# An fp6 linear layer's pairs moved into the attention heads' stage of a macaron block

## The reference

```
x = x + 0.5 * moe(layernorm(x));  x = x + attention(layernorm(x));  x = x + 0.5 * moe(layernorm(x))
x = x + 0.5 * fp6_linear(layernorm(x))                       # first use
x = x + heads(layernorm(x))                                  # 16 heads, causal, relative bias, its own layernorm inside
x = x + 0.5 * fp6_linear(layernorm(x))                       # second use, same weight and bias

fp6_linear(x): for each row and block of 32: s = max(max|x| / 7.5, 1e-30); q = nearest value of the e2m3 grid to x / s
               the same for the weight's rows;  out = (q * s) @ (qw * sw).T + bias
heads(x):      xn = layernorm(x) * gamma + beta;  q, k, v = xn @ W.T;  softmax(q k / 4 + rel[dist], causal) v;  @ Wo.T
```

## Time and profile before

| | us |
|---|---|
| median of 3 runs | 2751.59 |
| lowest, highest | 2748.57, 2754.42 |
| the profiled execution | 2777.85 |
| its span, first to last instruction | 2776.0 |
| first use of the fp6 layer | 194 (1544 to 1738) |
| heads | 860 (1738 to 2598) |
| second use of the fp6 layer | 178 (2598 to 2776) |

### The profile page before, as it was taken

One profiled execution on the slowest core, in us unless ns is written; L12 is line 12 of the kernel. 1 busy time (PEld: TensorE's weight loads), 2 busy tenths in 40 slices (PEclk: granted clock), 3 DMA queues, 4 the chain that ended last, 5 costly groups with the idle time before them and its releaser, 6 DMA issues.

```text
span 2776.0 us, 39998 instructions
## 1 busy us (share of the span) xinstructions
PE 2217.6 (80%) x13342; PEld 1613.4 (58%) x13342; DVE 1620.4 (58%) x4577; ACT 969.2 (35%) x1964; POOL 453.9 (16%) x402
## 2 busy tenths in 40 slices
PE   4489999908999857999994276378999999999476
PEld 2478888806888736888883144324444454444254
DVE  6744443353555675433444897266866766875695
ACT  4122233203333331232331331325555556556321
POOL 4320000040000134000003553411011011000242
PEclk8799999958999878999997555669999999999755
DMA  7110101020000122001002100242322323230001
GB/s 237 41 59 26 28 28 32 22 76 1 1 1 1 35 83 73 28 28 32 28 28 60 49 12 0 61 65 59 48 42 53 48 47 63 37 43 2 5 22 39
DMA packets 83735, 114.14 MB, mean 41 GB/s; under 512 B 12162, under 2 KB 74020, under 8 KB 80420
## 3 DMA queue, kind: packets, MB, share of 16 engines
q1 hardware_dynamic: 77396, 94.53, 15.5%
q0 software_dynamic: 6144, 17.05, 1.9%
HBM read 68.90 MB, written 42.64 MB: 40 GB/s over the span
## 4 chain that ended last, share of the span: by engine, by line
PE 63%; DVE 21%; ACT 5%; issue 5%; DMA 3%; POOL 2%; another core or an unknown queue 1%; SPq 0%; ACTq 0%; DVEq 0%; POOLq 0%
PE psum L774 9%; PE psum L776 9%; PE psum L775 9%; PE psum L122 5%; PE psum L2097 4%; PE psum L123 4%; PE psum L124 4%; PE psum L2076 4%; PE psum L2056 3%; PE psum L861 3%; PE psum L2080 3%; DVE junk L1961 2%; PE psum L1426 2%; DVE m L1949 1%; DVE stats L155 1%
## 5 line engine op out<-in xcount | busy, mean ns | idle before, releaser
L1898 ACT ACTIVATE pt<-psum 128x512 f32<-128x512 f32 (+3 forms) x768 | 338.9, 491 | 283.2 <-DVE psum L1987 196.2
L739 DVE SCALAR_TENSOR_TENSOR h<-psum,xg,sg 128x128 f32<-128x128 f32 x592 | 166.9, 345 | 415.2 <-PE psum L861 415.2
L774 PE MATMUL psum<-w_hi,xt_hi 128*128 (+1 forms) x720 | 286.3, 398 | 33.7 <-DVE xt_lo L704 33.7
L548 ACT ACTIVATE sg<-psum 128x512 f32<-128x512 f32 x180 | 107.6, 598 | 584.0 <-PE psum L776 543.0
L775 PE MATMUL psum<-w_lo,xt_hi 128*128 (+1 forms) x720 | 284.5, 395 | 0.0
L776 PE MATMUL psum<-w_hi,xt_lo 128*128 (+1 forms) x720 | 284.5, 395 | 0.0
L2056 PE MATMUL psum<-ks,qs 96*128 96x512 bf16 (+3 forms) x768 | 232.9, 342 | 49.7 <-DMA ks<-qk_scr 19.9
L2076 PE MATMUL psum<-qs,ks 99*128 99x512 bf16 (+3 forms) x768 | 236.8, 332 | 18.4 <-ACT pt L1898 11.4
L774 PE MATMUL psum<-w_hi,ht_hi 128*128 (+1 forms) x720 | 220.5, 306 | 8.3 <-DVE x L754 8.0
L1961 DVE CUSTOM_DVE_ANT_0 junk<-psum,band_q 128x256 bf16<-128x256 f32 (+1 forms) x512 | 204.8, 400 | 22.3 <-PE psum L2056 12.0
L776 PE MATMUL psum<-w_hi,ht_lo 128*128 (+1 forms) x720 | 205.9, 286 | 0.0
(11 more groups left out here) (281 smaller groups left out, 4884.4 us busy)
## 6 DMA issues: line engine op xcount, KB each, us to landing
xg<-w_dram SPq DMA_DIRECT2D x54, 256.0 KB, 3.3
qk_scr<-parts SPq DMA_DIRECT2D x32, 384.0 KB, 2.5
qs<-qk_scr SPq DMA_DIRECT2D x96, 128.0 KB, 7.0
ks<-qk_scr SPq DMA_DIRECT2D x96, 128.0 KB, 7.7
xg<-rows_in SPq DMA_DIRECT2D x74, 132.0 KB, 2.2
rows_out<-yb SPq DMA_DIRECT2D x74, 128.0 KB, 1.7
x<-x_dram SPq DMA_DIRECT2D x4, 1024.0 KB, 9.3
out_dram<-x SPq DMA_DIRECT2D x4, 1024.0 KB, 4.4
```

The lines of the kernel that those rows point to most:

```text
L739: ins = dve.scalar_tensor_tensor(out=h[i % 2][:, e, :], in0=u[:, e, :], scalar=xg[j % XSLOT][:, at:at + 1], in1=sg[i % 2][:, e, :], op0=AL ...
L774: pe.matmul(out, a[0], b[0], start=first, stop=False)
L1898: act.activation(pt[n % NPT][:, 0:q1 - q0], st_bank(n)[:, 0:q1 - q0], ACT.Exp).then_inc(*exped.up())
```

## The change

`linear` and `linear_order` are replaced by a class `Linear` with the steps of each engine, `pair_steps` (the steps of a pair, with `slack` empty rounds in two places) and `in_turn` (the rounds). `linear_first` is the first stage with the pairs of batches 0 and 1 only, 8 pairs. The other 24 pairs, 8 of the first use for batches 2 and 3 and 16 of the second, stand in the heads' order: a `fill` with two pairs in flight and five empty rounds in each of two places gives one round after each score step. In batches 0 to 2 it begins with the third unit, in batch 3 after the last batch's output step; 6, 6, 4 and 4 pairs are dealt to the four batches, and the last 4 pairs (batch 3 of the second use) follow the heads with one empty round. A batch of the second use is stored when its fourth pair is summed. The weight is quantised once.

Two sets of buffers for the pairs are laid over those of the projection: `xn`, `xt`, `parts`, `rests`. `rests` and `yd` become one buffer, and a third of the `pt` buffers is 384 columns wide instead of 512. ScalarE waits, before a pair's centring, for the projection and the writes from `parts`; before an output step it waits for the pairs' products. The `sum` of a pair (now `lin_sum`) follows `lin` by one round, where it was three; the second rounding has steps of its own (`round`, `even`) behind the empty rounds. A batch's projection starts when the last batch's conclusion has been written, not with it. The pairs' turns and products use the heads' ring of three banks.

The roots are made per batch, at `heads_stat` and `linear_stat` in the order, with Ln and Exp in place of Sqrt and a reciprocal, and two refinements in place of one.

```
+        def pair_steps(n, layer, pair, slack):
+
+            yield [("centre", n)]
+            for kind in ("amax", "scaled", "power", "shift"):
+                yield [(kind, n)]
+            for _ in range(slack):
+                yield []
+            yield [("round", n)]
+            yield [("even", n)]
+            yield [("least", n)]
+            yield [("requant", n)]
+            for _ in range(slack):
+                yield []
+            yield [("q_turn", n)]
+            yield [("q_low", n)]
+            yield [("lin", n)]
+            yield [("lin_sum", n)]
+            yield [("lin_collect", n)] if layer == 0 else [("lin_store", n)]
...
             for u in range(NU):
                 b, g = divmod(u, NHG)
                 if g == 0:
                     proj = project(b + 1) if b + 1 < BATCH else iter(())
+                    may_project, may_fill = b == 0, False
+                if g == (2 if b + 1 < BATCH else 0):
+                    fill = linear_fill(([("linear_stat", b - 1)] if b else []) + list(mine[b]), 5)
+                    may_fill = g == 2
...
-                    order.extend(next(tail, []))
-                    if step % 3 == 0:
+                    late = next(tail, None)
+                    order.extend(late or [])
+                    may_project, may_fill = may_project or late is None, may_fill or late is None
+                    if step % 3 == 0 and may_project:
                         order.extend(next(proj, []))
+                    if may_fill:
+                        order.extend(next(fill, []))
...
+                size = TILES * D
+                words = parts[:, :, :, :].rearrange("p a k s -> p (a k s)").bitcast(F32)
+                linear.begin(jobs, [
+                    Quantising(st, flat(xn)[:, 0:size], flat(xn)[:, size:2 * size], rests[0],
+                               flat(xt[0])[:, 0:size], flat(xt[1])[:, 0:size]),
+                    Quantising(st, rests[1], words[:, 0:size], words[:, size:2 * size],
+                               flat(xt[0])[:, size:2 * size], flat(xt[1])[:, size:2 * size])], mx_ring.bank)
...
+                def inverse_root(which, b):
+
+                    at = slice(b * BT, (b + 1) * BT)
+                    act.wait_ge(*S("variance")(roots[which, b] + 1))
+                    act.activation(sd[:, at], ve[:, at], ACT.Ln).then_inc(*S("logarithm").up())
+                    act.wait_ge(*S("logarithm")(roots[which, b] + 1))
+                    act.activation(recip[:, at], sd[:, at], ACT.Exp, scale=-0.5).then_inc(*S("root").up())
...
         with ExitStack() as stack:
-            tables = HeadTables(stack)
-            linear(False, tables)
-            attention_heads(tables)
-        linear(True)
+            tables, linear = HeadTables(stack), Linear(stack)
+            linear_first(tables, linear, 2)
+            attention_heads(tables, linear, 2)
```

553 lines of the change are left out of this document (313 added, 240 removed).

## The result

The changed kernel takes 2838.09 us (median of 4 runs, 2833.51 to 2840.95); the kernel before, on the same chip, 2750.08 (2748.53 to 2754.42). The ratio is 1.0316, 95% interval 1.0296 to 1.0335: 3.2% slower, where I had forecast 0.6% faster and a range that ended at 2788.

The account below looks back on a forecast made before the run. TensorE was taken to set the pace in the heads' stage, with VectorE 81% busy. First stage -72, roots +45, fills +142, collision -17 and end -114 gave -16: 2736 us from a median of 2751.6, range 2692 to 2788.

Parts of the forecast that it names:

- First stage: First use of the fp6 layer: keeping 8 of 16 pairs saves 74 us, less 2 for the earlier sum: -72.
- Roots: Per-batch roots by Ln and Exp: +6 at the heads' start, +24 in the loop, +15 for linear roots: +45.
- Collision: Projection's write behind a unit's loads in batches 1 and 2: twice 8.33 us of waiting goes, -17.
- End: Second use's 178 us stage goes; a root, four last pairs and the store take 64 us: -114.
- Fills: Twenty pairs in four stretches of the heads' loop: +100 floor from VectorE's work, +42 for product waits: +142.
- the two prices of a pair: A moved pair in the heads' stage: VectorE 6.6 us, or 7.6 with statistics; TensorE 3.3 us at full clock.
- 2.1 us for a product's piece: In the fills, VectorE's wait for a pair's 2.8 us of products costs 2.1 us each, 20 times: +42.
- The floor case: Rival: fills cost only VectorE's work beyond its free time, -42, and -8 for a shorter end; 2694 us, chance 0.17.
- the forecast's bubbles: VectorE's waits for pairs' products in the fills, limited by three banks of maxima: +42 over twenty pairs.
- The clock rival: Rival: TensorE falls to 1.2 GHz in the fills, deciding under a mean grant of 0.77; +57, 2793 us, chance 0.15.
- The late bias additions: Rival: VectorE's late bias additions in the fills hold ScalarE, then TensorE, 0.8 us each; +40, 2776 us, chance 0.15.
- 76 us more at the worst: Over 20 pairs, GpSimd operations fully stopping VectorE, 3.8 us a pair, could cost up to 76 us more.

Follow-up runs that it names:

- e12: Changed kernel with the first use in its own stage, only eight second-use pairs moved into the heads' stage, eight in a last stage; 1.0112 of the kernel before.
- e9: Kernel before with only the next batch's projection starting after the previous unit's output step, no pair moved; 1.0039 of the kernel before.
- e8: Changed kernel with all sixteen first-use pairs back in their own stage, the second use left moved; 1.0253 of the kernel before.
- e18: Kernel before plus 216 independent VectorE maxima and, in the same eight units, three pieces a unit of twelve TensorE products; 1.0540 of the kernel before.
- e13: Kernel before plus 216 independent VectorE maxima of about 0.69 us, 27 in each of eight units; 1.0395 of the kernel before.
- e7: Changed kernel with batch 2's four second-use pairs moved from units 12 and 13 to the middle of unit 14 on; 1.0294 of the kernel before.
- e14: Changed kernel with each score product issued twice in the units with pairs; 1.0333 of the kernel before.
- e2: Changed kernel with each score product issued three times in the eight units with pairs; 1.0413 of the kernel before.
- e5: Changed kernel without VectorE's bias additions in the eight units with pairs, ScalarE taking those scores from TensorE; 1.0215 of the kernel before.

## Why the prediction was wrong, step by step

- *First stage, -72 forecast:* 194 us became 114.3, -80. Right in kind, 8 us better.
- *Roots, +45:* the start +5.3 (107.5 for the 102.2 from 1738 to before's first maxima at 1840.2); batch 1 +5.6 (59.6 us between the first two maxima for 54.0); batches 2 and 3 +7.8 each; a linear root 6.2, from e12 (35.6 us in batch 1's stretch with a linear root, 28 in batch 2's without, less 1.4 for the place, if the pairs of the two cost the same). In all 5.3 + 5.6 + 15.6 + 18.6 = 45. Right. The double table load that the sum went by stands in the trace, 1.28 us each time:

```profile
1742.45 1.28 ACT L1874 ACT_TABLE_LOAD   x1
1743.75 0.21 ACT L1874 ACTIVATE std<-var_eps 128x8 f32<-128x8 f32 x1
1743.97 1.28 ACT L1876 ACT_TABLE_LOAD   x1
```

- *Collision, -17:* wrong in sign. e9 has it at +8. I had counted the wait that goes, twice 8.33 us of the chain where ScalarE waited 4.34, and not that the projection's rounds are pushed into a unit that had none.
- *End, -114:* 242.0 us from the last maxima became 134.0, -108. Near enough.
- *Fills, +142:* this is the step that failed. What is left of the +91 when the other terms have their measured sizes is 91 + 80 - 45 - 8 + 108 = 226 us, 11.3 a pair for 7.1. In units 2 to 5 it was 81 for six, 13.5 each.

Inside the fills the two prices of a pair were about right. Against e8, whose piece has the projection and the root in the same places, VectorE works 46.7 us more in units 2 to 5 (147.8 for 101.1), 7.8 a pair for my 7.6, and TensorE 21, 3.5 a pair for my 3.3. (The 6.9 us of the linear stage was luck in part: I had divided by the 7.97 us between two pairs of the first use. The second use's pairs end 8.47 us apart, 127.0 us from first to last, which makes it 7.4.)

The rule by which I put the two together, VectorE's work beyond its free time and 2.1 us for a product's piece, nearly comes out where nothing else is there: 135 us by the rule for e18, 145 measured. VectorE's free time takes in less than the rule says (e13, 107 us for 85), and a piece costs 1.5 us instead of 2.1. What failed is that I let a pair cost nothing beyond these two terms. I had no term for the clock ("about 1.00 for me") and none for the waits of the pair's steps on one another and of the attention on them. The twenty real pairs cost 226 us where I had 142. In units 2 to 5 they are 44 us longer than e18, of which 29 are clock and 21 idle time, with 6 less work. VectorE would have been busy 88% by my rule; it was 69%. The loads that should have been 60 us apart were so by 80.4 and 76.5 (first DMAs at 1857.74, 1938.15 and 2014.67). Where VectorE has hardly anything else to do (e7) four pairs and a root still cost 35 us, and two pairs in 76 us (e12) 9 us each. Of the 84 us that I missed, 10 lie in the rule itself, as e18 has it; how the rest parts between the clock and the order of the steps stays open. e14 and e2 win clock back and gain no time, and no run has real pairs at full clock without added work.

*The rivals.* The floor case went the wrong way: real pairs cost more than the forecast's bubbles, not less. The clock rival had a real mechanism: 96 us more are lost to the clock than in before, and I had argued it away with "long busy stretches always had 1.00". Its trigger was misjudged, too. I had it decide by the mean grant under 0.77; the mean stayed at 0.86, and the loss came all the same, since it falls on the stretches in which TensorE is the one that is waited for. The late bias additions are there in the waits, but taking them out gives back little more than their own work, 32 us for 27 (e5). A case in which both happen, clock and idle time together, I had not formed, and that is why the range ended 50 us too low.

The Trainium skill, "TensorE: Matmul & The Clock Gate" ("A second HAM failure mode: psum-queue depth-cycling"), tells of a kernel whose small idle gaps between groups of products let the clock swing between its levels, and that the throughput suffers by it. This case's trace agrees: between 1905 and 1960 of after the grant of the 5 us windows goes from 0.93 to 0.50, 1.00, 0.50 and 1.00 again. The Trainium skill, "SBUF — State Buffer" (two separate sides), has VectorE and GpSimd exclude each other for a whole instruction when VectorE's is in a two-port mode or has two inputs in SBUF. The row of e7 at 2671.74, an operation with one input, shows it stretched from 0.17 to 1.26 us, the length of GpSimd's. By that rule I had 76 us more at the worst; VectorE's busy time shows that it stayed small in sum, 7.8 us a pair for the 7.6 forecast.

## What to carry over

Work of independent pieces and the real steps have different prices. VectorE at 77% to 81% took independent operations at 0.76 to 0.77 us of time for each us put beside it, and with TensorE's pieces beside them that is 145 us, what the forecast had for its 20 pairs (142, with 140 us of VectorE work). The real pairs, with about the same work, cost 226. So a dummy of the same length and grain would have confirmed the wrong sign here. Before work is moved into such a stage, time a few real pieces of it there: e12's two pairs a stretch show 9 us each, and 20 x 9 = 180 in place of 142 turns the forecast of -16 into +22, the right sign. Work that fills a stage of its own at 8 to 9 us a piece is cheap against the 11 to 13 us that dense pairs cost beside attention, and a wait that is moved away is a gain only if what it held back doesn't land in a full place. No version here beats the kernel before: the best that keeps all work is e9, 0.4% slower.
